# Order of the q and k turns in a fused attention and windowed-transformer kernel: q, q, k, k with q scaled ahead of k

## The chip, the cores and the metric

The kernel runs on one core of a Trainium2 chip. The metric is device time in microseconds (us). The engines are TensorE (PE for matmuls, PEld for the loads of the stationary operand), VectorE (DVE), ScalarE (ACT), GpSimd (POOL) and SyncE (SP, whose queue issues the DMAs). Each engine works through its own list of instructions in order; semaphores are all that ties the lists together.

## The reference, cut to what matters

The input is 2048 tokens of width 128, in float32. It is normalised and feeds two branches, whose results are added to it. The first is an attention over all tokens with 16 heads of width 8. The second, on which the change bears, is a stack of six layers, each a windowed attention followed by a gated MLP. Of one layer's attention:

```python
def attn_layer(x, Wqkv, qs, ksc, Wo):
    q, k, v = jnp.split(x @ Wqkv, 3, -1)      # 16 heads of 64
    q = l2norm(q) * qs
    k = l2norm(k) * ksc
    q = q * cos * scale + rotate_half(q) * sin * scale
    k = k * cos * inv + rotate_half(k) * sin * inv
    out = local_attention(q, k, v)            # windows of 32, one window back
    return out @ Wo
```

## The kernel before, in words

Part A, up to about 750 us, computes the attention over all tokens. Part B computes the six layers. It cuts the 2048 tokens into 16 tiles of 128, so it has 96 tiles in all (`END`), and a chunk is four tiles, 24 in all. Every engine has a loop over `u` in which each stage is called with the tile that is due: the loop is a software pipeline, written out by hand, and the order of the calls in it is the order of the engine's list. Tiles are counted from 0 over all layers here; tile t of the text is `u` in a function's own argument.

The way of a tile through q and k:
- `project` (L1325 and on, products at L1334 to L1336): PE multiplies the tile with a third of Wqkv, two banks of PSUM for each of q, k and v. The float32 product is made of three products of cut operands.
- `squares` (L754, ACT) squares the raw q or k, and `square_sums` (L1020, DVE) sums it by head. From these ACT and POOL form the reciprocal norms (L764 to L768, then POOL L634, L641, L643).
- `rotate_cos` (L1038) and `rotate_sin` (L1049, L1050), both DVE, read the raw q or k from PSUM. The last of them frees the bank pair of q or k (semaphore `q_out` or `k_out`).
- `rotated` (L652, POOL) adds the two parts in SBUF, and `normalise` (L660, POOL) multiplies by the reciprocal norm. It raises `q_scaled` or `k_scaled`.
- `turn` (L1360, PE) transposes the scaled q or k, 128 columns at a time: a call has four transposes, so a tile has four calls, q_turn0, q_turn1, k_turn0 and k_turn1. Each waits for `q_scaled` or `k_scaled` and for its PSUM bank.
- `turned_q` (L776) and `turned_k` (L785 into this tile's keys, L788 into the next tile's window back), both ACT, move the turned halves to SBUF, in the order q, q, k, k.
- `score` (L1376, L1381, PE) needs all four. DVE takes the maxima (L1069), ACT the 16 exponentials (L805, `exponentials`), DVE the sums (L1076) and their reciprocals (L1083), POOL scales (L614), DVE transposes blocks (L1061), SP moves them, and PE multiplies with v (`values`, L1397). ACT moves that result out (L796), and `output` (L1409, PE) multiplies with Wo.

In one round of PE's loop the turns belong to tile t = u - 2. Ahead of them stand the output product of tile t - 3 and the q and k products of tile t + 1. Behind them stands the v product of tile t + 1. `mean` (L1418, part of the MLP's layer norm) stands ahead of the last turn in one round in four: at tiles 6, 10, ... 94, and once more in the tail. The up products of a chunk (also L1334 to L1336, from `xl_cut`, whose low half is L1139 on DVE) follow the v product in the rounds of tiles 5, 9, ... The variance product (L1426) and the down product (L1448) follow it in the rounds of tiles 3, 7, ...

Banks of PSUM are shared between stages. `BANKS` gives the banks for even and odd tiles, and `bank_users` walks through the stages in PE's order, to say for each use whose reading out it must wait for:

```python
BANKS = {"q": ((4, 5), (4, 5)), "k": ((2, 3), (2, 3)), "v": ((0, 1), (4, 5)),
         "q_turn0": ((4,), (4,)), "q_turn1": ((1,), (5,)), "k_turn0": ((6,), (6,)),
         "k_turn1": ((0,), (7,)), "values": ((6, 7), (6, 7)), "output": ((7,), (7,)),
         "score": ((0, 1), (0, 1)), "mean": ((7,), (7,)), "var": ((4,), (4,)),
```

So q_turn0 always waits until DVE has read the raw q of the next tile (L1050). For an even tile, q_turn1 (bank 1) and k_turn1 (bank 0) wait for the exponentials of the tile before (L805), and the v product behind them (banks 4 and 5) waits for ACT's first reading of turned q. For an odd tile, q_turn1 (bank 5) waits for the same as q_turn0, and the v product (banks 0 and 1) waits for the exponentials.

POOL's round is: low half of x (L607), scaling of probabilities (L614), tables (L627), `rotated` of k, the reciprocal norms, `normalise` of k, `normalise` of q, `rotated` of the next tile's q.

Of the kernel before, what the change touches and what calls it, by code (L numbers as in the profile page):

```python
# [104 lines left out]
def tile(x):  # L105
    return x if 0 <= x < END else None


def chunk(x):
    c, r = divmod(x - 3, 4)  # L110
    return c if r == 0 and 0 <= c < CHUNKS else None


def dense_turn(x):
    g, r = divmod(x - 22, 8)
    return g if r == 0 and 0 <= g < NC else None


def late(x):
    c = chunk(x)  # L120
    return c if c is not None and c >= CHUNKS - NC else None
# [15 lines left out]
def banks_of(stage, unit):  # L137

    return (0, 1) if stage == "up2" and unit == CHUNKS - 2 else BANKS[stage][unit % 2]


def bank_users():

    users, last = {}, {}

    def take(stage, unit):
        if unit is not None:
            of = banks_of(stage, unit)
            users[stage, unit] = [last[b] for b in of if b in last]
            last.update({b: (stage, unit) for b in of})  # L150

    for u in range(FIRST, LAST):
        take("score", tile(u - 3))
        take("finish", late(u - 12))
        take("q", tile(u - 1))
        take("values", tile(u - 5))
        take("k", tile(u - 1))
        take("output", tile(u - 5))
        take("k_turn0", tile(u - 2))
        take("q_turn0", tile(u - 2))  # L160
        take("q_turn1", tile(u - 2))
        take("mean", chunk(u - 5))
        take("k_turn1", tile(u - 2))
        take("v", tile(u - 1))
        take("up0", chunk(u - 8))
        take("up2", chunk(u - 8))
        take("var", chunk(u - 6))
        take("down", chunk(u - 10))
        take("att", dense_turn(u))
        take("up1", chunk(u - 8))  # L170
    return users
# [18 lines left out]
def memory(nc, ctx, d):  # L190
# [79 lines left out]

    m.e_turn = exp_turns()
    m.users = bank_users()
    return m

# [9 lines left out]
def place(u):  # L284
    layer, i = divmod(u, NT)
    return layer, i, slice(i * P, (i + 1) * P)


def chunk_cols(g, skew=0):
    return slice(g * CH + skew, (g + 1) * CH + skew)  # L290
# [45 lines left out]
def wait_part_a(w, s):  # L336
    w.wait_ge(s["skew"], 2 * NC)
    w.wait_ge(s["pv"], H * NT * NC)
    for i in range(3):
        w.wait_ge(s[f"E_out{i}"], len(range(i, H * NT * NC + H, 3)))  # L340
    w.wait_ge(s["sc_max"], 2 * H * NT)
    w.wait_ge(s["o_ev"], H)
    w.wait_ge(s["ld_o0"], 16 * NC * H)
    w.wait_ge(s["ld_o1"], 16 * NC * H)
    w.wait_ge(s["z_low"], 2 * NC)
    w.wait_ge(s["idb"], 1)
    w.wait_ge(s["st_cut"], 32 * len(CUTS))
    w.wait_ge(s["cut"], 2 * len(CUTS))
# [250 lines left out]
def gpsimd_b(e, w, m, s):  # L599
    view = lambda a: a.rearrange("p (h d) -> p h d", h=H)  # L600

    def low_x(u):
        if u is None:
            return
        layer, i, c = place(u)
        w.wait_ge(s["x_hi"], u + 1)
        e.tensor_tensor(m.x_cut[u % 2][:, 1, :], m.stream[0][:, c], m.x_cut[u % 2][:, 0, :], ALU.subtract).then_inc(s["x_lo"], 1)  # L607

    def scale_probs(u):
        if u is None:  # L610
            return
        pb = m.pr[u % 2]
        w.wait_ge(s["sm_rec"], u + 1)
        e.tensor_tensor(pb[:, :, :, :], pb[:, :, :, :],  # L614
                        m.mxB[:, 2, :].unsqueeze(1).unsqueeze(3).to_broadcast([P, 2, H, WIN]), ALU.mult).then_inc(s["pnorm"], 1)

    def rotary(u):
        if u is None:
            return
        layer, st = u // NT, u % 2  # L620
        w.wait_ge(s[f"ld_rot{st}"], 16 * (u // 2 + 1))
        w.wait_ge(s[f"ld_gains{layer % 2}"], 96 * (layer // 2 + 1))
        w.wait_ge(s["rotq_c"], u - 1)
        w.wait_ge(s["q_out"], u - 1)
        w.wait_ge(s["rotk_c"], u - 1)
        w.wait_ge(s["k_out"], u - 1)
        e.tensor_tensor(m.rt[st][:, :, :], m.rot[st][:, :, :], m.gains[layer % 2][:, :, :], ALU.mult).then_inc(s["rt"], 1)  # L627

    def root_slope(u):
        if u is None:  # L630
            return
        c, t, r = [b[:, :] for b in m.rs[u % 2]]
        w.wait_ge(s["rB_sq"], u + 1)
        e.tensor_tensor(t, t, c, ALU.mult).then_inc(s["rB_t"], 1)  # L634

    def root_fix(u):
        if u is None:
            return
        c, t, r = [b[:, :] for b in m.rs[u % 2]]
        w.wait_ge(s["rB_t"], u + 1)  # L640
        e.tensor_scalar(t, t, -0.5, 1.5, ALU.mult, ALU.add).then_inc(s["rB_f"], 1)  # L641
        w.wait_ge(s["rB_f"], u + 1)
        e.tensor_tensor(r, r, t, ALU.mult).then_inc(s["rB_r"], 1)  # L643

    def rotated(u, i):
        if u is None:
            return
        n, tc = "qk"[i], m.tcs[u % 2][i]
        w.wait_ge(s[f"rot{n}_c"], u + 1)
        w.wait_ge(s[f"rot{n}_s"], u + 1)  # L650
        w.wait_ge(s[f"{n}_out"], u + 1)
        e.tensor_tensor(tc[:, :], tc[:, :], m.ts[i][:, :], ALU.add).then_inc(s[f"rot{n}"], 1)  # L652

    def normalise(u, i):
        if u is None:
            return
        n, tc = "qk"[i], view(m.tcs[u % 2][i][:, :])
        w.wait_ge(s[f"rot{n}"], u + 1)
        w.wait_ge(s["rB_r"], u + 1)
        e.tensor_tensor(tc, tc, m.rs[u % 2][2][:, i * H:(i + 1) * H].unsqueeze(2).to_broadcast([P, H, DH]),  # L660
                        ALU.mult).then_inc(s[f"{n}_scaled"], 1)

    wait_part_a(w, s)
    for i in range(2):
        e.memset(m.k_T[i][:, :, 0:WIN], 0.0).then_inc(s["zeroB"], 1)
    for u in range(FIRST, LAST):
        low_x(tile(u))
        scale_probs(tile(u - 3))
        rotary(tile(u))
        rotated(tile(u - 1), 1)  # L670
        root_slope(tile(u - 1))
        root_fix(tile(u - 1))
        normalise(tile(u - 1), 1)
        normalise(tile(u - 1), 0)
        rotated(tile(u), 0)


# [652 lines left out]
def tensor_b(e, w, m, s):  # L1330
# [20 lines left out]
    def turn(u, i, hf):  # L1351
        if u is None:
            return
        name = f"{'qk'[i]}_turn{hf}"
        bank = banks.one(name, u).rearrange("p (a b) -> p a b", b=P)
        w.wait_ge(s["k_scaled" if i else "q_scaled"], u + 1)
        banks.wait_free(w, name, u)
        for j in range(4):
            b = 4 * hf + j
            t = e.transpose(bank[:, j, :], m.tcs[u % 2][i][:, b * P:(b + 1) * P], m.ident[:, :])  # L1360
        t.then_inc(s[f"turn{i}{hf}"], 1)
# [50 lines left out]
    def mean(c):  # L1412
        if c is None:
            return
        layer, g = divmod(c, NC)
        w.wait_ge(s["y_out"], 4 * c + 4)
        banks.wait_free(w, "mean", c)
        e.matmul(banks.one("mean", c), m.ones[:, :], m.stream[1][:, chunk_cols(g)], start=True,  # L1418
                 stop=True).then_inc(s["mean_mm"], 1)

    def variance(c):
        if c is None:
            return
        w.wait_ge(s["lnsq"], c + 1)
        banks.wait_free(w, "var", c)
        e.matmul(banks.one("var", c), m.ones[:, :], m.lnb[:, :], start=True, stop=True).then_inc(s["var_mm"], 1)  # L1426
# [31 lines left out]
    def finish(c):  # L1458
        if c is None:
            return  # L1460
        bank = banks.one("finish", c).rearrange("p (j f) -> p j f", f=P)
        w.wait_ge(s["down_out"], c + 1)
        banks.wait_free(w, "finish", c)
        for j in range(CH // P):
            o = c % NC * CH + j * P
            t = e.transpose(bank[:, j, :], m.att[:, o:o + P], m.ident[:, :])
        t.then_inc(s["fin_T"], 1)

    for u in range(FIRST, LAST):
        score(tile(u - 3))  # L1470
        finish(late(u - 12))
        project(tile(u - 1), 0)
        values(tile(u - 5))
        project(tile(u - 1), 1)
        output(tile(u - 5))
        turn(tile(u - 2), 1, 0)
        turn(tile(u - 2), 0, 0)
        turn(tile(u - 2), 0, 1)
        mean(chunk(u - 5))
        turn(tile(u - 2), 1, 1)  # L1480
        project(tile(u - 1), 2)
        up_product(chunk(u - 8), 0)
        up_product(chunk(u - 8), 2)
        variance(chunk(u - 6))
        down_product(chunk(u - 10))
        dense_output(dense_turn(u))
        up_product(chunk(u - 8), 1)
# [62 lines left out]
```

## Time and profile before

| | |
|---|---|
| median of 3 runs | 2282.62 us (2280.07 to 2282.78) |
| the profiled execution | 2277.0 us |
| its span in the profile | 2275.2 us |
| PE, PEld busy | 92%, 57% |
| DVE, ACT, POOL busy | 87%, 78%, 58% |
| mean granted TensorE clock | 0.974 |
| from the first turn to the last (part B) | 760.5 to 2214 us |

The span is what the profiler saw from the first to the last instruction; the execution's own time is 1.8 us more. A row of a timeline gives the start (us from the span's start), the length in us, engine, line, operation, result and inputs, shape, and how many instructions are merged in it. A bracket gives the idle time of the engine ahead of it and what ended that. A merged row runs from the first start to the last end; matmuls overlap, so a row's end lies after the next row's start.

### The profile page before, as it was taken

To read this page: it belongs to the slowest core of one execution; us is meant where nothing else is said; L and a number is where in the kernel's file an instruction comes from. 1 tells how busy PE (TensorE), PEld (TensorE's weight loads), DVE (VectorE), ACT (ScalarE), POOL (GpSimd) and SP (SyncE) were. 2 spreads that over 40 slices of the span, in tenths; PEclk is the share of its full clock that TensorE was granted. 3 is DMA by queue.
4 is the path that set the end of the run, shared out by engine and by line. 5 is a ranking of instruction groups with operands and counts; after the bars stand their busy time and mean duration, and the time that the engine had idled before them with its cause. 6 is when DMAs were issued, how large, how long until landed. Compare 5 with 4: busy or idle time off the path is not lost. (4 is left out here: it accounts for less than half of the span.)

```text
span 2275.2 us, 69842 instructions
## 1 busy us (share of the span) xinstructions
PE 2103.4 (92%) x28313; PEld 1287.8 (57%) x28313; DVE 1984.4 (87%) x2379; ACT 1770.7 (78%) x4234; POOL 1311.7 (58%) x1084
## 2 busy tenths in 40 slices
PE   5999999999998689999999999999999999999986
PEld 2122222222221477777777777677777777777764
DVE  7999999999990788989898999888898999899984
ACT  3388888888887577878787888788787878788873
POOL 4201101111100788878787888787787878888870
PEclk8699999999999799999999999999999999999998
DMA  2322222221220233353434334443335333533331
GB/s 43 98 61 77 79 62 90 67 79 47 62 78 8 59 87 75 83 145 84 104 84 126 99 93 104 113 103 86 82 85 141 85 92 85 139 86 98 84 89 52
DMA packets 167798, 194.12 MB, mean 85 GB/s; under 512 B 87414, under 2 KB 107508, under 8 KB 167476
## 3 DMA queue, kind: packets, MB, share of 16 engines
q1 hardware_dynamic: 167220, 189.65, 32.0%
q8 instruction: 223, 3.65, 0.7%
q14 instruction: 99, 0.81, 0.1%
q10 hardware_dynamic: 256, 0.00, 0.0%
HBM read 56.98 MB, written 25.42 MB: 36 GB/s over the span
## 5 line engine op out<-in xcount | busy, mean ns | idle before, releaser
L988 DVE TENSOR_REDUCE mx<-S_ps 128x1 f32<-128x1024 f32 x512 | 601.7, 1219 | 25.5 <-PE S_ps L1288 20.0
L736 ACT ACTIVATE PT<-E_ps 128x512 f32<-128x512 f32 x1024 | 533.4, 603 | 102.3 <-PE E_ps L1297 99.8
L652 POOL TENSOR_TENSOR tc<-tc,ts 128x1024 f32<-128x1024 f32 x192 | 463.1, 2412 | 28.8 <-DVE ts L1050 28.2
L660 POOL TENSOR_TENSOR tc<-tc,rs 128x1024 f32<-128x1024 f32 x192 | 362.7, 1910 | 13.7
L1288 PE MATMUL S_ps<-KS,QS 48*128 48x512 bf16 x1024 | 321.2, 400 | 9.9 <-DVE mx L988 4.7
L805 ACT ACTIVATE pr<-B_ps,mxB 128x64 f32<-128x64 f32 x1536 | 323.8, 371 | 1.6 <-DVE mxB L1069 1.6
L1297 PE MATMUL E_ps<-QS,KS 64*128 64x512 bf16 x1024 | 317.5, 383 | 7.4 <-ACT PT L736 5.2
L594 POOL CAST w_cut_b<-w_raw_b 128x512 fp32r<-128x512 f32 (+1 forms) x48 | 27.6, 574 | 512.5 <-DMA w_raw_b<-in_Wqkv 380.0
L1334 PE MATMUL B_ps<-w_qkv,x_cut 128*128 128x512 f32 x576 | 259.8, 451 | 30.7 <-POOL x_cut L607 8.8
L1305 PE MATMUL O_ps<-PT,va 128*32 128x512 f32 x2048 | 274.1, 607 | 0.0
L1297 PEld LDWEIGHTS E_ps<-QS,KS 64*128 64x128 bf16 x1024 | 79.4, 94 | 338.5 <-ACT PT L736 257.9
L614 POOL TENSOR_TENSOR pr<-pr,mxB 128x1024 f32<-128x1024 f32 x96 | 183.8, 1915 | 138.3 <-DVE mxB L1083 138.3
L1038 DVE TENSOR_TENSOR tc<-B_ps,rt 128x1024 f32<-128x1024 f32 x192 | 234.8, 1223 | 29.9 <-ACT nrm L754 23.7
L754 ACT ACTIVATE nrm<-B_ps 128x1024 f32<-128x1024 f32 x192 | 208.1, 1084 | 37.2 <-PE B_ps L1336 36.7
L1020 DVE TENSOR_REDUCE ss<-nrm 128x16 f32<-128x1024 f32 x192 | 232.0, 1208 | 0.0
L1335 PE MATMUL B_ps<-w_qkv,x_cut 128*128 128x512 f32 x576 | 231.6, 402 | 0.0
L1336 PE MATMUL B_ps<-w_qkv,x_cut 128*128 128x512 f32 x576 | 230.9, 401 | 0.3 <-issue 0.3
L1360 PE MATMUL B_ps<-ident,tc 128*128 128x128 f32 x1536 | 204.9, 277 | 22.4 <-POOL tc L660 10.8
L1397 PE MATMUL B_ps<-xy,vs 128*64 128x64 f32 x3072 | 196.3, 228 | 19.7 <-issue 9.0
L1360 PEld LDWEIGHTS B_ps<-ident,tc 128*128 128x128 f32 x1536 | 173.1, 142 | 52.3 <-issue 19.7
L1397 PE MATMUL B_ps<-xy,v 128*64 128x64 f32 x3072 | 192.4, 225 | 9.1 <-issue 9.1
L1397 PEld LDWEIGHTS B_ps<-xy,vs 128*64 128x64 f32 x3072 | 168.1, 140 | 57.4 <-issue 57.2
(181 smaller groups left out, 3971.3 us busy)
## 6 DMA issues: line engine op xcount, KB each, us to landing
xy<-pc SPq DMA_DIRECT2D x768, 64.0 KB, 2.0
vs<-v SPq DMA_DIRECT2D x96, 384.0 KB, 3.7
Wqkv_cut<-w_cut_b SPq DMA_DIRECT2D x72, 256.0 KB, 2.4
w_qkv<-Wqkv_cut SPq DMA_DIRECT2D x36, 512.0 KB, 7.3
rot<-in_rot SPq DMA_DIRECT2D x96, 128.0 KB, 2.6
vs<-v SPq DMA_DIRECT2D x96, 128.0 KB, 3.8
w_raw_b<-in_Wqkv SPq DMA_DIRECT2D x36, 256.0 KB, 2.9
W_cut<-w_cut_b SPq DMA_DIRECT2D x24, 170.5 KB, 2.5
```

The source lines that it names most:

```text
L652: e.tensor_tensor(tc[:, :], tc[:, :], m.ts[i][:, :], ALU.add).then_inc(s[f"rot{n}"], 1)
L660: e.tensor_tensor(tc, tc, m.rs[u % 2][2][:, i * H:(i + 1) * H].unsqueeze(2).to_broadcast([P, H, DH]), ALU.mult).then_inc(s[f"{n}_scaled"], 1)
L736: e.activation(m.PT[n % NPT][:, :], turns.bank("probs", n)[:, :], ACT.Exp).then_inc(turns.sem("probs", n), 1)
L805: a = e.activation(pb[:, :, h, :], sc[:, h, :, :], ACT.Exp, bias=m.mxB[:, 0, h:h + 1], scale=1.0)
L988: e.tensor_reduce(m.mx[h % 2][:, i, hf:hf + 1], m.S_ps[n % 2][:, :, :], AX.XY, ALU.max).then_inc(s["sc_max"], 1)
L1038: e.tensor_tensor(view(m.tcs[u % 2][i][:, :]), raw, wide(m.rt[u % 2][:, 2 * i, :], DH), ALU.mult).then_inc(s[f"rot{n}_c"], 1)
L1288: mm = e.matmul(m.S_ps[n % 2][:, c, :], m.QS[sl][rows, i * P:(i + 1) * P], m.KS[sl][rows, k:k + CH], start=True, stop=True)
L1297: e.matmul(turns.bank("probs", n)[:, :], m.KS[sl][rows, j * P:(j + 1) * P], m.QS[sl][rows, chunk_cols(c)], start=True, stop=True).then_inc ...
L1305: e.matmul(m.O_ps[VC * c:VC * (c + 1), :], m.va[:, j, h, :], m.PT[n % NPT][:, :], start=(j == 0), stop=(j == NT - 1)).then_inc(s["pv"], 1)
L1334: e.matmul(bank, left[0], right[0], start=True, stop=False)
L1360: t = e.transpose(bank[:, j, :], m.tcs[u % 2][i][:, b * P:(b + 1) * P], m.ident[:, :])
L1397: mm = e.matmul(bank[at, j, :, b, :], v[:, d:d + DH], m.xy[u % 2][:, b, :, par * NP + j, :], start=(b == 0 and j % (NP // 2) == 0), stop=T ...
```

## The change

The two calls of q's turns move ahead of the first of k's turns in PE's loop, and in the walk that assigns the waits for banks. In POOL's loop the scaling of q moves ahead of the scaling of k. No instruction is added or removed, no bank is changed, and ACT's order of reading out stays as it is. `normalise(u, 0)` is q, `turn(u, 0, half)` is q.

```diff
--- before.py
+++ after.py
@@ -156,9 +156,9 @@
         take("values", tile(u - 5))
         take("k", tile(u - 1))
         take("output", tile(u - 5))
-        take("k_turn0", tile(u - 2))
         take("q_turn0", tile(u - 2))
         take("q_turn1", tile(u - 2))
+        take("k_turn0", tile(u - 2))
         take("mean", chunk(u - 5))
         take("k_turn1", tile(u - 2))
         take("v", tile(u - 1))
@@ -670,8 +670,8 @@
         rotated(tile(u - 1), 1)
         root_slope(tile(u - 1))
         root_fix(tile(u - 1))
+        normalise(tile(u - 1), 0)
         normalise(tile(u - 1), 1)
-        normalise(tile(u - 1), 0)
         rotated(tile(u), 0)
 
 
@@ -1473,9 +1473,9 @@
         values(tile(u - 5))
         project(tile(u - 1), 1)
         output(tile(u - 5))
-        turn(tile(u - 2), 1, 0)
         turn(tile(u - 2), 0, 0)
         turn(tile(u - 2), 0, 1)
+        turn(tile(u - 2), 1, 0)
         mean(chunk(u - 5))
         turn(tile(u - 2), 1, 1)
         project(tile(u - 1), 2)
```

## Rows read from the trace of the kernel before

**Rows 1.** Busy time by stretch: length, PE, PEld, DVE, ACT, POOL, granted clock, DMA share, GB/s.
```profile
760.00:2214.00 1454.00, 1358.46 (x23648) 1075.91 (x23649) 1297.29 (x1668) 1176.59 (x3093) 1186.47 (x949) 0.99 0.38 96
```
**Rows 2.** The turns' line L1360: duration, and PE's idle time ahead of it by what ended it.
```profile
L1360 PE MATMUL B_ps<-ident,tc x1536: 272/273/477, 760.5 to 2213.8; 128*128 128x128 f32 x192
...
  POOL tc L660: 30.3, 41
...
  ACT pr L805: 12.8, 37
```
**Rows 3.** Timeline, odd tile 43: the turns, POOL's scaling, the v product.
```profile
1416.32 1.90 POOL L660 TENSOR_TENSOR tc<-tc,rs 128x1024 f32<-128x1024 f32 x1
...
1417.91 1.91 PE L1360 MATMUL B_ps<-ident,tc 128*128 128x128 f32 x16
...
1419.58 0.48 PE L1334 MATMUL B_ps<-w_qkv,x_cut 128*128 128x512 f32 x1
```
**Rows 4.** Timeline, even tile 42 with the mean product: from the turns to the scores.
```profile
1404.65 1.83 PE L1360 MATMUL B_ps<-ident,tc 128*128 128x128 f32 x12
...
1405.82 0.42 PEld L1360 LDWEIGHTS B_ps<-ident,tc 128*128 128x128 f32 x4 [0.37 <-ACT pr L805]
...
1407.17 0.60 PE L1360 MATMUL B_ps<-ident,tc 128*128 128x128 f32 x4
...
1407.53 0.48 PE L1334 MATMUL B_ps<-w_qkv,x_cut 128*128 128x512 f32 x1
...
1408.11 0.77 ACT L785 ACTIVATE k_T<-B_ps 128x512 f32<-128x512 f32 x1
...
1408.59 0.55 ACT L788 ACTIVATE k_T<-B_ps,carry 128x128 f32<-128x128 f32 x1
...
1408.79 0.39 PE L1336 MATMUL B_ps<-w_qkv,x_cut 128*128 128x512 f32 x1
...
1409.28 0.39 PE L1376 MATMUL B_ps<-mask_bf,pick_bf 64*128 64x512 bf16 x2
```
**Rows 5.** The turns of the first (tile 6) and the last (tile 94) such round.
```profile
847.33 1.84 PE L1360 MATMUL B_ps<-ident,tc 128*128 128x128 f32 x12
...
2197.64 1.83 PE L1360 MATMUL B_ps<-ident,tc 128*128 128x128 f32 x12
```
**Rows 6.** Timeline, even tile 44 without the mean product: first turns, v product.
```profile
1435.78 0.60 PE L1360 MATMUL B_ps<-ident,tc 128*128 128x128 f32 x4
...
1438.35 0.50 PE L1334 MATMUL B_ps<-w_qkv,x_cut 128*128 128x512 f32 x1 [0.28 <-ACT q_T L776]
```
**Rows 7.** Timeline, odd tile 33: turns, POOL, the v product, xl_cut and the up product.
```profile
1265.71 0.60 PE L1360 MATMUL B_ps<-ident,tc 128*128 128x128 f32 x4
...
1266.37 2.38 POOL L652 TENSOR_TENSOR tc<-tc,ts 128x1024 f32<-128x1024 f32 x1
...
1267.75 0.48 PE L1334 MATMUL B_ps<-w_qkv,x_cut 128*128 128x512 f32 x1
...
1267.99 1.31 DVE L1139 TENSOR_TENSOR xl_cut<-xl,xl_cut 128x512 fp32r<-128x512 f32 x1
...
1269.36 0.19 PEld L1334 LDWEIGHTS B_ps<-xl_cut,w 128*128 128x128 f32 x1 [0.40 <-DVE xl_cut L1139]
```
**Rows 8.** Timeline, odd tile 21: DVE's reading of q, turns, the up product.
```profile
1078.23 0.67 DVE L1050 TENSOR_TENSOR ts<-B_ps,rt 128x512 f32<-128x512 f32 x1
...
1079.05 1.50 PE L1360 MATMUL B_ps<-ident,tc 128*128 128x128 f32 x12 [0.61 <-POOL tc L660]
...
1082.06 0.19 PEld L1334 LDWEIGHTS B_ps<-xl_cut,w 128*128 128x128 f32 x1 [0.55 <-DVE xl_cut L1139]
```
**Rows 9.** All DVE's xl_cut instructions: duration in ns, shortest, median, longest.
```profile
L1139 DVE TENSOR_TENSOR xl_cut<-xl,xl_cut x24: 681/1248/2005, 895.9 to 2258.2; 128x512 fp32r<-128x512 f32 x24
```
**Rows 10.** Timeline, PE at the start of a layer, after tile 30; PE's turns of tile 95.
```profile
1227.60 0.47 PE L1334 MATMUL B_ps<-w_qkv,x_cut 128*128 128x512 f32 x1 [0.62 <-DMA w_qkv<-Wqkv_cut]
...
2212.59 1.53 PE L1360 MATMUL B_ps<-ident,tc 128*128 128x128 f32 x12 [0.40 <-POOL tc L660]
```

## The prediction

> **What bounds the kernel now.** I read the page first. PE is busy 92% of the span, but DVE, ACT and POOL are at 87, 78 and 58%, so no single share settles it, and I went by stretches. The change touches only the stretch from 760 to 2214 us. There PE is busy 1358 of 1454 us at a granted clock of 0.99, DVE 1297, ACT 1177, POOL 1186 [rows 1]. PE has 96 us of gaps, one us a tile, and of those only a part stands ahead of the turns. The view of line L1360 says what part: 30.3 us in 41 gaps ended by POOL's scaling, and 12.8 us in 37 gaps ended by ACT's exponentials [rows 2]. The first sum is what the change can win, the second what it can make longer. Then I went through the timeline, tile by tile.
>
> An undisturbed tile shows the scale. Its 16 turns stand in one row of 1.91 us without a gap, one turn takes 0.27 us, so they start (1.91 - 0.27) / 15 = 0.11 us apart and a call of four costs 0.44 us [rows 2, 3]. POOL's second scaling ends at 1416.32 + 1.90 = 1418.22, that is 0.31 us after the first turn, and q's first call is due 0.44 us after it. So k_turn0 already covers the whole wait for q here. Tiles 3, 7, ... 91 look like this or have POOL still earlier.
>
> **The change part by part.** It adds no work: four calls of 0.44 us and two scalings of 1.90 us stay what they are. Nothing moves on SP, DVE or ACT, and no DMA. On POOL, q is ready one scaling (1.90 us) sooner and k as much later. What is queued behind both, the next tile's `rotated`, starts at the same time. So everything is decided by which of three releases comes last on PE: the scaling, DVE's reading of the next raw q, or ACT's exponentials.
>
> *Odd tiles where q waits for POOL.* In tile 33 POOL's second scaling ends where `rotated` (L652) begins behind it, at 1266.37 or 0.66 us after the first turn, and q_turn0 waits for it. The v product starts at 1267.75, 2.04 us after the first turn at 1265.71; undisturbed it is 1419.58 - 1417.91 = 1.67 [rows 3, 7]. With q first, the second scaling is needed 0.88 us after the first turn instead of 0.44, so this gap of 0.37 goes. I find 13 such tiles, all in the rounds of the up products (first tile 13, last tile 89), worth 4.3 us together at 0.03 to 0.48 us each. But what is late next? In tile 33 the up product waits for `xl_cut`, which ends at 1267.99 + 1.31 = 1269.30, while PE had been idle 0.40 us in its weight loads [rows 7]. That DVE instruction takes 0.68 us at its shortest and 1.25 at the median [rows 9], and it is long where POOL's L652 lies across it: here L652 ends at 1268.75 and DVE 0.55 us later. Neither of the two moves with the order of the scalings. So I take nothing for these tiles, with 4.3 us as the other bound: the v product comes 0.37 us sooner and the up product at the same time.
>
> The Trainium skill has a rule for this, in "SBUF — State Buffer", section "SBUF: two separate sides": a DVE instruction with two SBUF inputs and a GpSimd instruction that reads SBUF take one port pair by an exclusive lock, and the later one blocks until the other is done. The trace agrees in that the DVE instruction ends a fixed 0.55 us behind POOL's. By the rule these 13 tiles give nothing; without it, all 4.3 us.
>
> *Odd tiles where q waits for DVE too.* In tiles 21, 73 and 93 q_turn0 waits 0.61 us on PE's row [rows 8]. The gap bears POOL's name, but DVE's reading of the next q ends as late, at 1078.23 + 0.67 = 1078.90, 0.15 us before q's turns start. With q first, q_turn0 still waits for DVE, and k_turn0, which ran under this wait, now runs behind: +0.44 us on the v product. The up product behind it had been waiting for `xl_cut` already: 12 turns from 1079.05 are 1.31 us, the v product's six products 1.50 (1407.53 to 1409.03 in tile 42, below), so PE was free at 1081.86 and started at 1082.06 [rows 8]. These 0.20 us absorb nearly half; I take 0.2 us each, +0.6 us for three, between 0 and 1.3. Among the first three tiles, where the pipeline fills, tiles 1 and 2 have long waits of this kind; I take +0.5 us for the three, between 0 and 3 x 0.44 = 1.3.
>
> *Even tiles.* These carry the sum. q_turn1 (bank 1) waits for the exponentials. In tile 42 the weight load of q_turn1 starts at 1405.82 after an idle 0.37 us ended by ACT, and the first 12 turns take 1.83 us instead of 0.27 + 11 x 0.11 = 1.48 [rows 4]. The exponentials do not depend on the turns: they end 1.12 us after the first turn in nearly all even tiles. With q first, q_turn1 is due 0.44 us after the first turn, not 0.88. It still starts at 1405.82, and k_turn0 comes behind it and no longer under the wait. So the calls end 0.44 us later.
>
> What this costs depends on what stands behind. Without the mean product (tiles 4, 8, ...) the v product waits 0.28 us on PE's row for ACT's first reading of turned q: it starts at 1438.35, 2.57 us after the first turn at 1435.78, [rows 6]. If q_turn1 starts 1.17 us after the first turn, as in tile 42, three calls bring PE to the v product at 1.17 + 3 x 0.44 = 2.49, still under 2.57. I take 0 for these, because ACT's chain (exponentials, squares, q) does not move; without that cover it would be 0.44 us for each of 24.
>
> With the mean product, 23 tiles, there is no such cover: mean stands between q_turn1 and k_turn1, and the v product follows k_turn1 at once, at 1407.53 [rows 4]. The first and the last of them show the same 1.84 and 1.83 us [rows 5]. The v product comes 0.44 us later, at 1407.97. Behind it come the scores, and they start at 1409.28, 0.14 us after ACT's last reading of turned k (1408.59 + 0.55 = 1409.14). PE was free at 1409.03, one product (0.24 us) after the start of the last, 1408.79. After the change PE is free at 1409.47. ACT's second reading of k, now at 1408.11, needs k_turn1, which ends at 1407.77 + 0.44 = 1408.21, so ACT is 0.12 us late and would let the scores go at 1409.40. PE is the later: the scores start some 0.20 us later, 0.20 and not 0.44. This is the term I trust most in kind, and its bounds are 0 and 0.44. From the scores on PE runs without a gap to `values`, and DVE, ACT and POOL behind it wait for PE, so the 0.20 us stays in the time. Not everywhere: at the start of each new layer, after tiles 14, 30, 46, 62 and 78, the q product waits for its weights (0.62 us after tile 30 [rows 10]), whose DMA was started before the turns, and after three others (54, 58, 94) `values` is late for other reasons. That leaves 15 tiles: 15 x 0.20 = 3.0 us.
>
> *The last tile.* Tile 95 has q waiting 0.40 us for POOL on PE's row, on the chain that ended last, with no up product behind it [rows 10]: -0.4 us.
>
> **Sum:** 3.0 + 0.6 + 0.5 - 0.4 = +3.7 us. The profiled execution took 2277.0 us with a span of 2275.2; it would become 2280.7. The median of the runs, 2282.6, lies 5.6 us above the profiled one, and I put the same difference on it: 2286.3 us, +0.16%. A measurement of this kernel tells about 0.2% (4.6 us) from no change, so the likeliest verdict is no change, leaning to slower.
>
> **The rivals.** (1) *The full 0.44 us, slower.* If the 0.44 us of the 23 mean tiles goes through whole, because the scores do not have the slack I read from ACT's last reading, the sum is 23 x 0.44 + 1.3 + 1.3 - 0.4 = +12.3 us, 2294.9. It decides at 0.31 us a tile (with 15 tiles, above +4.6 us in all; with 23 tiles at 0.20 us). For it: PE is the fullest engine, and the gaps that absorb are few. Against: the 0.25 us between PE's being free and the scores stand in the timeline of every such tile. Chance 0.27.
>
> (2) *The gains come through, faster.* If `xl_cut` does not hold PE, because it ends sooner once the up product is asked for sooner, the 13 tiles give 4.3 us, and if ACT's slack swallows the 23 tiles wholly, nothing stands against it: -4.3 - 0.4 = -4.7, 2277.9 us. For it: 30.3 us of gaps bear POOL's name. Against: most of them are in the filling of the pipeline and under `xl_cut`. Chance 0.10.
>
> (3) *No effect beyond tenths.* The turns shift inside their round and every stage behind them is released by ACT or DVE as before: 0 to +1 us, 2283. Chance 0.13. My forecast has 0.50.
>
> Gaps ended by nothing that the profile shows (19.7 us before the turns in the view of L1360) can shift by a few us with any reordering. They widen every case.
>
> **How the numbers follow.** Faster by over 0.2%: rival 2 is at the bound, 0.10, with 0.02 from scatter: 0.12. Slower: rival 1, 0.27, and a tail of the forecast, 0.06: 0.33. Within: 0.55. The range takes in the forecast, rival 3 and most of rival 1, whose median case with partial cover is near 2292: 2280 to 2293.
>
> **What would show it.** In the changed profile tile 42's kind has the first four turns, a gap of about 0.6 to 0.8 us ended by ACT's L805, then eight turns, mean, four turns, and the v product about 3.3 us after the first turn instead of 2.88. The scores follow 4.8 us after the first turn instead of 4.63. The idle time of L1360 ended by L805 grows from 12.8 to some 30 us, and that ended by POOL's L660 falls by 10 us or more. In rounds like tile 33's the v product moves up 0.37 us and the up product not at all. The forecast is wrong if the distance of the scores grows by 0.4 us or by nothing, or if the up product follows the v product.

## The result, and the profile after

| | before | after |
|---|---|---|
| median of 20 runs each, same chip | 2281.1 us (2276.42 to 2283.28) | 2287.73 us (2277.76 to 2299.18) |
| profiled execution | 2277.0 us, span 2275.2, clock 0.974 | 2296.88 us, span 2295.1, clock 0.968 |

The ratio is 1.0028, with a 95% interval of 1.0017 to 1.004: +6.4 us, between 3.9 and 9.1. The point forecast was 2286.3 us and the range 2280 to 2293, so the time lies inside. The median is slower by a little more than the 0.2% that the text called the least that can be told, and the interval reaches to both sides of that bound.

Two things need care. The profiled execution is one of the slowest of the changed kernel, 9 us above its median. And its runs spread over 21 us where those of the kernel before spread over 7. So I read in it only distances inside single tiles, and took a second profile of both kernels (below). Busy time by stretch, [rows 1] of the changed kernel, same columns:

```profile
760.00:2234.00 1474.00, 1362.31 (x23649) 1086.02 (x23650) 1296.91 (x1668) 1178.06 (x3094) 1185.90 (x949) 0.98 0.37 95
```

The stretch is 20 us longer. No engine has work to match: PE's busy time grew 4 us, DVE's, ACT's and POOL's by 1.5 us at most. The other 16 us are gaps of PE. Two more lines of the view of L1360 before, the one of [rows 2]:

```profile
  issue: 19.7, 59
...
  DVE ts L1050: 7.2, 9
```

The same view of the changed kernel shows who releases the turns now:

```profile
L1360 PE MATMUL B_ps<-ident,tc x1536: 272/273/446, 761.9 to 2233.2; 128*128 128x128 f32 x192
...
  ACT pr L805: 42.5, 69
  issue: 41.1, 72
  DVE ts L1050: 23.7, 20
  POOL tc L660: 0.6, 2
```

POOL's 30.3 us are down to 0.6, so the change does what it says. ACT's 12.8 us have become 42.5, DVE's 7.2 have become 23.7, and those that nothing in the profile ends, 19.7, have become 41.1. These sums are larger than PE's idle time: the view adds the gaps on the row of the matmuls (PE) to those on the row of the weight loads (PEld), so that one wait can stand in it twice. Row by row, of POOL's 30.3 us before 10.8 stand on the matmuls' row and 19.6 on the loads'. Of ACT's 42.5 us after, 16.9 stand on the matmuls' row, and all 41.1 us of "issue" on the loads'. Next the timeline of tile 42, the answer to [rows 4]:

```profile
1411.61 0.60 PE L1360 MATMUL B_ps<-ident,tc 128*128 128x128 f32 x4
...
1412.78 1.09 PE L1360 MATMUL B_ps<-ident,tc 128*128 128x128 f32 x8 [0.57 <-ACT pr L805]
...
1413.71 1.02 PE L1418 MATMUL B_ps<-stream,ones 128*128 128x512 f32 x2
...
1414.57 0.60 PE L1360 MATMUL B_ps<-ident,tc 128*128 128x128 f32 x4
...
1414.92 0.48 PE L1334 MATMUL B_ps<-w_qkv,x_cut 128*128 128x512 f32 x1
...
1415.20 0.64 ACT L785 ACTIVATE k_T<-B_ps 128x512 f32<-128x512 f32 x1
...
1415.70 0.40 ACT L788 ACTIVATE k_T<-B_ps,carry 128x128 f32<-128x128 f32 x1
...
1416.50 0.39 PE L1376 MATMUL B_ps<-mask_bf,pick_bf 64*128 64x512 bf16 x2
```

Four turns, a gap of 0.57 us ended by the exponentials, eight turns, the mean product, four turns. The v product starts 3.31 us after the first turn (2.88 before). The scores start 1416.50 - 1411.61 = 4.89 us after it (4.63 before): 0.26 us later. ACT's second reading of k (L785) starts 3.59 us after the first turn, 0.13 later than before, but it is as much shorter (0.64 instead of 0.77 us). Its last reading ends at 1416.10, 4.49 us after the first turn and exactly as far as before. The scores start 0.40 us behind that end, where it was 0.14: now PE is the last, with the v product's last matmul at 1416.17.

### The profile page after: what moved, and what is told of

Same layout as the page of the kernel before. It is cut to its first block and busy times, and to the rows that moved or that the text cites. A ratio compares the mean times of both kernels' runs of the same rounds, so it can differ in the third digit from the quotient of the medians.

```text
span 2295.1 us, 69842 instructions
## 1 busy us (share of the span) xinstructions
PE 2107.0 (92%) x28313; PEld 1297.1 (57%) x28313; DVE 1984.1 (86%) x2379; ACT 1771.7 (77%) x4234; POOL 1311.2 (57%) x1084
## 3 DMA queue, kind: packets, MB, share of 16 engines
q8 instruction: 223, 3.65, 0.7%
## 5 line engine op out<-in xcount | busy, mean ns | idle before, releaser
L652 POOL TENSOR_TENSOR tc<-tc,ts 128x1024 f32<-128x1024 f32 x192 | 463.3, 2413 | 37.3 <-DVE ts L1050 36.8
L1334 PE MATMUL B_ps<-w_qkv,x_cut 128*128 128x512 f32 x576 | 261.0, 453 | 24.3 <-POOL x_cut L607 8.9
L1360 PE MATMUL B_ps<-ident,tc 128*128 128x128 f32 x1536 | 198.6, 277 | 41.2 <-DVE ts L1050 23.7
L1360 PEld LDWEIGHTS B_ps<-ident,tc 128*128 128x128 f32 x1536 | 172.4, 142 | 67.4 <-issue 41.1
```

What stands on the lines that cost most here:

```text
L1334: e.matmul(bank, left[0], right[0], start=True, stop=False)
```

## The experiments

Twelve kernels ran, each timed in five rounds beside the kernel before on the same chip. Theories 1 and 2 stood at the start, the third came before e5. **Theory 1**: the order costs time in the 23 tiles with the mean product, where q_turn1 and not k_turn0 stands at ACT's exponentials. **Theory 2**: it costs where PE's gaps ahead of the turns, once split by k_turn0, become one long gap, and the granted clock falls behind it. **Theory 3**: beside the cost in the mean tiles, part of the loss is in stalls inside the scores that the profile puts down to nothing, and where these fall hangs on where the code of PE lies.

### One half undone, one half alone

**e1**: PE in the order q, k, q, k; POOL as in the change. Here and in e3 the walk that assigns the waits for banks follows PE's order.

```diff
         turn(tile(u - 2), 0, 0)
-        turn(tile(u - 2), 0, 1)
         turn(tile(u - 2), 1, 0)
+        turn(tile(u - 2), 0, 1)
```

> Changed kernel, but PE turns q, k, q, k, so that k_turn0 again runs while q_turn1 waits for the exponentials; POOL's order stays q, k. Theory 1 (the loss is the cover that q_turn1's wait lost in the 23 mean tiles, plus the first tiles): the scores of tile 42 start 4.64 us after the first turn again instead of 4.89, values 7.97 instead of 8.22, the steps of 0.25 us vanish, and the time comes back to before, +0 to +1.5 us. Theory 2 (most of the loss is half-clock stretches behind longer single gaps ahead of q_turn0, which waits for DVE in either order): +4 to +8 us, with 10 or more half-clock stretches and a spread of the runs of over 10 us, as in the changed kernel.

Measured: 2282.58 us, ratio 1.0015 (1.0001 to 1.0029), +3.4 us. Timeline of tile 42 in e1:

```profile
1405.83 1.82 PE L1360 MATMUL B_ps<-ident,tc 128*128 128x128 f32 x12
...
1407.00 0.42 PEld L1360 LDWEIGHTS B_ps<-ident,tc 128*128 128x128 f32 x4 [0.37 <-ACT pr L805]
...
1408.35 0.60 PE L1360 MATMUL B_ps<-ident,tc 128*128 128x128 f32 x4
...
1410.46 0.39 PE L1376 MATMUL B_ps<-mask_bf,pick_bf 64*128 64x512 bf16 x2
```

With k_turn0 back under the wait the scores stand 4.63 us behind the first turn again. The 0.26 us are thus the lost cover of q_turn1, and about half of the loss goes with them. The rest, e1's +3.4 us, lies in neither theory's range (0 to 1.5 and 4 to 8). Its runs stay within 10 us (2276.9 to 2286.89).

**e2**: the changed kernel, with q_turn1 of even tiles in bank 5, which the exponentials do not use.

```diff
-         "q_turn0": ((4,), (4,)), "q_turn1": ((1,), (5,)),
+         "q_turn0": ((4,), (4,)), "q_turn1": ((5,), (5,)),
```

> Changed kernel with q_turn1 of even tiles in bank 5 instead of bank 1, so that it waits for DVE's reading of q (done before) and not for the exponentials; k_turn1 still waits for them. Theory 1: q, q, k run without a gap (0, 0.44, 0.87), the v product of tile 42 waits for ACT's second reading of q at about 3.05 us, and the scores start at 4.6 to 4.7 us instead of 4.89: +0 to +1.5 us against before. Theory 2: no difference to the changed kernel, +4 to +8 us.

Measured: 2290.65 us, ratio 1.0051 (1.0031 to 1.0071), +11.6 us. This missed: it should have cured the tiles, and it is slower than the change itself. The timeline of e2 for tile 42:

```profile
1411.12 1.47 PE L1360 MATMUL B_ps<-ident,tc 128*128 128x128 f32 x12
...
1414.28 0.47 PE L1334 MATMUL B_ps<-w_qkv,x_cut 128*128 128x512 f32 x1 [0.39 <-ACT q_T L776]
```

and the idle time ahead of the products' line L1334 in e2, by what ended it:

```profile
  ACT q_T L776: 53.4, 83
```

Before, that line had 15.7 us in 38 gaps. The wait for the exponentials has gone (12 turns in 1.47 us), but the v product of an even round writes banks 4 and 5. Bank 5 now holds turned q, and v waits for ACT's second reading of it, in tiles with and without mean (in tile 4, without, v starts 3.17 instead of 2.58 us after the first turn). The scores stand at 4.73 instead of 4.63 us in the mean tiles and at 4.74 instead of 4.64 us in tile 4. I had looked at who writes bank 1 and not at who writes bank 5 next.

**e3** has the new order on PE alone, **e4** on POOL alone.

```diff
 e3, PE
-        turn(tile(u - 2), 1, 0)
         turn(tile(u - 2), 0, 0)
         turn(tile(u - 2), 0, 1)
+        turn(tile(u - 2), 1, 0)
 e4, POOL
+        normalise(tile(u - 1), 0)
         normalise(tile(u - 1), 1)
-        normalise(tile(u - 1), 0)
```

> Only PE's half of the change: PE turns q, q, k, k, but POOL still scales k first, so q_turn0 needs the second scaling at once. Theory 1: in tiles 3, 7, ... q_turn0 waits 0.3 us for POOL (+0.3 us each, 23 tiles), in 13 tiles of the up products the whole of 0.5 to 0.7 us, of which the wait for xl_cut takes part: with the 0.25 us of the mean tiles, +10 to +17 us against before. Theory 2: the same gaps, and more half-clock stretches still: over +17 us.

> Only POOL's half of the change: q is scaled first, but PE still turns k first, so k_turn0 needs the second scaling at once. Theory 1: mean tiles as before (scores at 4.64 us), +0.3 us in each of tiles 3, 7, ..., about +0.25 us in the 13 tiles of the up products: +6 to +11 us. Theory 2: as in theory 1 by the gaps, and a spread of the runs of over 10 us.

Measured: e3 2292.49 us, ratio 1.0057 (1.0038 to 1.0077), +13.0 us, as expected; e4 2282.17 us, 1.0017 (1.0005 to 1.0029), +3.9 us, less than expected. Idle time ahead of L1360, of e3 and then of e4:

```profile
  POOL tc L660: 47.6, 50
  ACT pr L805: 42.6, 67
```

```profile
  POOL tc L660: 55.7, 84
...
  ACT pr L805: 16.8, 54
```

Either half alone makes POOL the last releaser more often than the 30.3 us of before. In e4, PE's first turn is still k's, now scaled last: 25 us more of gaps bear POOL's name, and the time grows by 3.9. On the matmuls' row alone POOL's gaps grow by 12.1 us (22.9 after 10.8) and DVE's fall by 6.0 (1.2 after 7.2), so about half of it is a wait that only changed its name. In e3, ACT's 42.6 us alone equal those of the change: they come with PE's order.

### New order in the tiles with mean only, and in the others only

```diff
+def q_first(t):
+    return chunk(t - 3) is not None
...
+def turn_order(t):
+    return ("q_turn0", "q_turn1", "k_turn0") if q_first(t) else ("k_turn0", "q_turn0", "q_turn1")
...
-        turn(tile(u - 2), 1, 0)
-        turn(tile(u - 2), 0, 0)
-        turn(tile(u - 2), 0, 1)
+        for stage in turn_order(u - 2):
+            turn(tile(u - 2), "qk".index(stage[0]), int(stage[-1]))
```

This is **e5**; POOL and the list of banks follow the same function, and **e6** has `is None` for the other 73 tiles.

> The new order (PE q, q, k, k and POOL q first) in the 23 tiles with the mean product alone, the old order in the other 73. Theory 1 (the loss sits in the cover that q_turn1's wait lost in the mean tiles): scores at 4.89 and values at 8.22 us there, +3 to +5 us against before, that is about all of the change's loss but the first tiles. Theory 3 (the loss sits elsewhere: in the filling of the pipeline, in DVE's release of q_turn0 and in the stalls inside the scores that it moves): the same distances in the timeline, but less than half of the change's +6.4 us, under +3 us.

> The complement: the new order in the 73 tiles without the mean product, the old one in the 23 with it. Theory 1: 0 to +1.5 us, values of tile 42 at 7.97 us. Theory 3: +3 to +6 us, with the stalls at the scores of tile 4 (about 825 us) and tiles 50 to 56 that the changed kernel's trace has and the one before has not.

Measured: e5 2285.18 us, ratio 1.0025 (1.0009 to 1.0041), +5.7 us (2.1 to 9.3); e6 2283.74 us, 1.0016 (1.0002 to 1.003), +3.6 us (0.5 to 6.8). Tile 42 in e5 and then in e6 (their lines are numbered 7 higher):

```profile
1405.16 0.60 PE L1367 MATMUL B_ps<-ident,tc 128*128 128x128 f32 x4
...
1406.34 1.09 PE L1367 MATMUL B_ps<-ident,tc 128*128 128x128 f32 x8 [0.58 <-ACT pr L812]
...
1410.06 0.39 PE L1383 MATMUL B_ps<-mask_bf,pick_bf 64*128 64x512 bf16 x2
```

```profile
1408.63 1.84 PE L1367 MATMUL B_ps<-ident,tc 128*128 128x128 f32 x12
...
1413.28 0.39 PE L1383 MATMUL B_ps<-mask_bf,pick_bf 64*128 64x512 bf16 x2
```

4.90 us in e5, 4.65 in e6. Theory 1 gives 23 x 0.26 = 6.0 us, and e5 has 5.7. The granted clock is not what makes it: its median over the runs is 0.973 in e5 and in the kernel beside it. But a stall of 1.38 us in tile 50, of the kind shown below, is in e5's profile too, so the 5.7 us need not be the mean tiles' alone. And e6, where the order predicts nothing or a small gain, is not at zero. What it loses does not repeat from tile to tile. Measured from scores to scores, each kind of tile (by its place in the chunk) differs from before by a median of 0.02 us or less, while single tiles differ by -1.3 to +3.4 us.

### The same kernels once more, and moved in the instruction stream

Because the loss in single tiles looked accidental, both kernels were run again (**e7** the change, **e8** the kernel before), and both with 64 or 128 satisfied waits on PE ahead of the loop, which move its later code and change no order.

```diff
+    for _ in range(64):
+        e.wait_ge(s["fold_mm"], 9)
     for u in range(FIRST, LAST):
         score(tile(u - 3))
```

> The changed kernel once more, for a second profile beside the first (span 2295.1 us) and for runs on the same chip: +4 to +9 us. Theory 1: its distances in the mean tiles are 4.89 and 8.22 us again. Theory 3: the stalls of 1.8 to 2 us inside the scores at 825 and between 1540 and 1630 us stand at the same places again, so they belong to the order and are not chance.

> The kernel before once more, for a second profile: 0 us, within 0.1%. Theory 3: none of the stalls named for the changed kernel at 825 us, and at most two between 1540 and 1630 us; if they come and go, the profile of one run can't carry that theory.

> The changed kernel with 64 waits on a semaphore long reached put ahead of part B on PE (32 instructions in the program), so that all of PE's later code sits further back; nothing else. Theory 3 (beside the 0.26 us in the mean tiles, the rest of the loss is stalls inside the scores that hang on where PE's instruction loads fall): the stalls at tile 4 (about 824 us) and tile 50 (about 1540 us) vanish or move to other tiles, and the median moves by 2 us or more, either way; the mean tiles keep 4.89 and 8.22 us. Theory 1 (the order alone): the same stalls at the same tiles, the median within 1.5 us of 2287 us.

> As before it with 128 such waits (64 instructions). Theory 3: a third pattern of stalls, with tile 4 and tile 50 not both stalled, and a median 2 us or more from one of the other two. Theory 1: the same as the changed kernel within 1.5 us.

> The kernel before with the same 64 waits. Theory 3: its median moves by 2 us or more from 2279 us, most likely upwards, as its own placing is among the better ones; the mean tiles keep 4.64 and 7.97 us, and the changed kernel with the same padding is 4 to 8 us slower than it. Theory 1: within 1.5 us of 2279 us.

> The kernel before with 128 such waits. Theory 3: as for 64, another pattern; over the three placings the difference between the orders averages some 6 us, 23 tiles by 0.26 us. Theory 1: within 1.5 us of 2279 us, and the changed kernel 6 to 8 us above it in every placing.

| placing | old order | new order | difference |
|---|---|---|---|
| as it is | e8 2278.93, 0.9995 (0.9984 to 1.0007) | e7 2286.94, 1.0036 (1.002 to 1.0053) | +8.0 (4 to 14) |
| 64 waits | e11 2283.65, 1.002 (1.0003 to 1.0036) | e9 2287.56, 1.0022 (1.0011 to 1.0033) | +3.9 (-1 to 7) |
| 128 waits | e12 2287.31, 1.0021 (1.0008 to 1.0035) | e10 2292.19, 1.005 (1.0038 to 1.0062) | +4.9 (3 to 8) |

The last column is the difference of the medians, with 95% of what it gives when the 5 to 12 runs of each are drawn again. By the ratios it would be +9.3, +0.5 and +6.6 us. The new order costs 5.6 us by the mean of the medians' differences and 5.5 by that of the ratios, near the 6.0 of the mean tiles, but the second row by itself doesn't tell it from zero, and the third rests on only five runs of e10. Part of the first row is the clock: the median granted clock is 0.971 in e7's runs and 0.973 in e8's, and e7's own runs go by 2.2 us for 0.001, so some 4 of the 8.0 us, an estimate, go with it. Moved by 64 waits, the change went from a ratio of 1.0036 to 1.0022, by 128 to 1.005, that is -3.2 and +3.2 us, though its median moved by only +0.6 and by +5.2; theory 3 asked for 2 or more. The old order, moved, is itself 4.6 to 4.8 us slower by its ratios. The waits at the head are not what costs: the first turn of tile 0 starts at 760.1 and 760.3 us in e11 and e12, and at 760.5 and 759.6 in the two profiles of before. What was moved costs later.

Where, the timelines tell. Tile 4's scores on PE, of the change, of e7 and of e8:

```profile
823.02 1.38 PE L1381 MATMUL B_ps<-k_T,q_T 64*32 64x64 f32 x116
...
826.26 0.33 PE L1381 MATMUL B_ps<-k_T,q_T 64*32 64x64 f32 x12 [1.85 <-issue]
```

```profile
821.65 1.38 PE L1381 MATMUL B_ps<-k_T,q_T 64*32 64x64 f32 x116
...
824.74 0.33 PE L1381 MATMUL B_ps<-k_T,q_T 64*32 64x64 f32 x12 [1.70 <-issue]
```

```profile
821.01 1.48 PE L1381 MATMUL B_ps<-k_T,q_T 64*32 64x64 f32 x128
```

In both runs of the change PE stops after the same 116 of 128 score matmuls for 1.70 to 1.85 us, and the view names nothing that ends the gap. e3 stops there too (1.58 us), and e2 one matmul earlier (2.08). The kernel before doesn't stop there in either profile, nor do e1, e4 to e6 or e9 to e12. Tile 50 has a second such place, after matmul 114 (1.87 us in the change, 1.97 in e7), and so have e3 (1.36) and e5 (1.38), which have the new order in this tile; before, e1, e2, e4 and e6 have none there, and e9, the new order moved by 64 waits, has none:

```profile
1536.42 1.09 PE L1360 MATMUL B_ps<-ident,tc 128*128 128x128 f32 x8 [0.57 <-ACT pr L805]
...
1540.46 1.49 PE L1381 MATMUL B_ps<-k_T,q_T 64*32 64x64 f32 x128
```

In e9 the 0.57 us ahead of the turns stay and the stall is gone. Summed over the kernel, PE's waits of this kind within L1381 (us, times, longest), of the change and of e8:

```profile
PE B_ps L1381 <- issue: 13.7, 9, 2.0
```

```profile
PE B_ps L1381 <- issue: 9.3, 6, 1.9
```

e7 has 12.9 us and the first profile of before 9.1, so some 4 us of the profiled difference lie here. Most such places belong to no order: tiles 52, 54 and 55 stall after matmuls 125, 124 and 126 in the change and in the kernel before, in both profiles of each. e8, of which at most two between 1540 and 1630 us were expected, has four. The moved kernels have their stalls in new places, most of them the same in both orders, among them the products' line L1334. There e11 has its longest (e9 has 4.30 us at this place, e10 and e12 have 5.30 and 5.56 us at another place of this line; the longest in the two profiles of before is 3.16):

```profile
1725.80 0.59 PE L1334 MATMUL B_ps<-w_qkv,x_cut 128*128 128x512 f32 x1 [5.29 <-issue]
```

**What ends the stalls** can be read from the DMA packets. One packet of the instruction queue falls into 823.5 to 826.5 us of the change:

```profile
q8 instruction: 1, 0.02, 2.3%
```

It runs from 823.54 to 824.65 us, and PE goes on at 826.26, 1.61 us after its end. In e7 PE goes on 1.44 us after the end of such a packet. In e8 the packet ahead of this matmul ended at 818.54, 3.6 us before PE came to it, and the next one starts only behind it; the same holds for before, e1 and e4 to e6, by 2.5 to 4.0 us. In tile 50 the packet ends 0.1 to 0.8 us after PE has come to the place in the four kernels that stall after matmul 114, and 3.4 us or more ahead in the other six whose code isn't moved. And it holds everywhere: of the 14 profiles' 235 gaps of over 0.4 us on PE's matmul row between 760 and 2215 us that the view calls "issue", each ends 1.20 to 1.67 us after the end of a packet of the instruction queue, though such packets come only every 7.7 us on average. So the stalls fit a wait for instructions whose packet came late. Why it comes late in one order or placing and not in another stays open.

These 235 gaps add up to 27.5 and 25.0 us in the two profiles of before, 31.7 and 28.4 in those of the change, 27.3 in e9, 30.4 in e10, 32.3 in e11 and 29.5 in e12. With 6.0 us for the mean tiles, the difference between the orders would be 9.4 us from e8 to e7, where the spans differ by 10.4, and 1.0 from e11 to e9, where they differ by 1.0. From the first profile of before to that of the change it would be 10.2 of 19.9, and from e12 to e10 6.9 where 3.4 were measured: there something else changed too.

**Theory 2** has one clear place, tile 40. The turns on PE and the next 4.5 us in the change:

```profile
1380.68 2.66 PE L1360 MATMUL B_ps<-ident,tc 128*128 128x128 f32 x16 [2.39 <-DVE ts L1050]
```

```profile
1381.00:1385.50 4.50, 4.50 (x21) 3.80 (x19) 4.42 (x9) 3.14 (x7) 3.89 (x3) 0.62 0.45 119
```

and the stretch of before that answers to it:

```profile
1373.50:1378.00 4.50, 2.88 (x18) 2.34 (x18) 4.42 (x8) 4.50 (x15) 3.94 (x3) 1.00 0.74 197
```

PE sits idle 2.39 us in one piece for DVE's reading of raw q. Then the granted clock is 0.62 on average, part of it at 1.2 GHz and part at 2.4, and 16 turns take 2.66 us. Before, k_turn0 stood inside the wait and left 1.69 us of it ahead of q, and the clock stayed at 1.00. From tile 39's first turn to tile 41's it is 2.6 us longer, 0.90 of which is a stall in tile 40's scores, and the next tile gives 1.1 of it back. e7, e6 and e2 show the same (gaps of 2.59, 2.54 and 2.51 us, granted clock 0.67 over e7's 1376.00 to 1380.50), e5 and e8, with the old order here, do not. But e1 and e3 had gaps of 2.26 and 2.69 us in this place and kept 1.00. In e9 and e10 the gap itself was shorter (1.47 and 1.28 us), and the clock stayed up. In e11, with the old order, the half clock comes later in the tile, behind a stall of 1.91 us in the scores. So the place fits the theory, and neither the order nor the length of the gap decides it.

As a theory of the whole loss it falls, for e1 kept the long waits for DVE and lost half of the loss. Between 785 and 2215 us the clock record has 1.2 GHz for 20 and 24 us in the two profiles of before, 44 and 25 in those of the change, and 34 and 40 in e11 and e12, whose order is the old one. So moving the code, too, came with more time at 1.2 GHz.

## Why the prediction was right, and where it was off

**Tiles with mean: right in place and kind, too small.** The text took +0.20 us for the scores and got +0.26. It had ACT 0.12 us late, with its second reading of k at the scores. ACT's second reading did start 0.13 us later, but it was 0.13 us shorter, and its chain kept its end at 4.49 us. PE is the later one, as the text had it, and the scores start 0.26 us later. The text let them start the moment PE is free; in the changed trace they start 0.09 us behind that (last product 1416.17 + 0.24, scores 1416.50), and this is about what the step was short by. The larger error is the count. I let the time of five layer starts and three others be absorbed, and took 15 tiles: 3.0 us. Ten tiles with nothing else in them each have a period longer by 0.21 to 0.26 us in both pairs of profiles (before and the change, e8 and e7). All 23 at 0.26 us make 6.0 us, and e5, which changes only these, measured +5.7. So the mis-sized term is 15 x 0.20 = 3.0, which is 23 x 0.26 = 6.0 to the accuracy that e5 gives, 2.1 to 9.3, with tile 50's stall in it. Whether each of the eight excepted tiles pays the 0.26 can't be read: in the layer starts and in tiles 54 and 94 the period moves by more than 1 us between kernels of the same order (tile 46: +2.4 and +1.2 us in the two profiles of the change, +3.3 in e11).

**Tiles without mean: zero, right.** Tile 44, [rows 6], after the change:

```profile
1443.79 1.94 PE L1360 MATMUL B_ps<-ident,tc 128*128 128x128 f32 x16 [0.62 <-DVE ts L1050]
...
1445.57 0.50 PE L1334 MATMUL B_ps<-w_qkv,x_cut 128*128 128x512 f32 x1
```

q_turn0 comes first and waits for DVE, a wait that k_turn0 used to fill. The text didn't have that wait, but its cover held. Counted from the end of the output product ahead of the turns, v starts at 2.40 us (2.41 before), and over all 23 tiles of this kind the median of the scores' start is 4.48 us in both. The bound of 0.44 us each for 24 tiles didn't come.

**Tiles with an up product: almost no gain, right in the sum, not in its reason.** Tile 33, [rows 7], after the change:

```profile
1270.94 1.91 PE L1360 MATMUL B_ps<-ident,tc 128*128 128x128 f32 x16
...
1271.28 2.39 POOL L652 TENSOR_TENSOR tc<-tc,ts 128x1024 f32<-128x1024 f32 x1
...
1272.61 0.48 PE L1334 MATMUL B_ps<-w_qkv,x_cut 128*128 128x512 f32 x1
...
1273.24 0.98 DVE L1139 TENSOR_TENSOR xl_cut<-xl,xl_cut 128x512 fp32r<-128x512 f32 x1
...
1274.28 0.19 PEld L1334 LDWEIGHTS B_ps<-xl_cut,w 128*128 128x128 f32 x1 [0.45 <-DVE xl_cut L1139]
```

The v product starts 1.67 us after the first turn instead of 2.04, the 0.37 us of the text. PE then still waits for `xl_cut`. That ends at 1274.22, again 0.55 us behind POOL's L652, which ends at 1273.67. Counted from the first turn, the up product starts at 3.34 us instead of 3.65, so here it followed the v product, which was a sign against the forecast. The text held that L652 doesn't move with the order. It did: it starts 0.34 us after the first turn instead of 0.66, and DVE's instruction, which ends 0.55 us behind it, came to its end sooner and was shorter (0.98 instead of 1.31 us). Tiles 65 and 81 are like it, in e7 as well. Measured from the scores ahead, the 13 up products start 1.0 us sooner in sum in the change and 0.7 in e7, of 4.3, and these three tiles make 1.0 in both. Even that isn't the tile's own order: e5 has it in tile 33 with the old order (3.30 us), and e6 doesn't with the new one (3.65). Rival 2, -4.7 us, is out.

That xl_cut's instruction is tied to POOL's is shown. In the 14 profiles it starts 245 times while L652 runs, and in 238 it ends 0.54 to 0.55 us after L652, whether it took 0.68 us or 2.0. Where no instruction of POOL lay across its start, it took 0.68 to 0.69 us. This is what the lock of the Trainium skill ("SBUF — State Buffer", "SBUF: two separate sides") describes, and the traces agree.

**Tiles 21, 73, 93: +0.6, measured about zero.** Tile 21, [rows 8], after the change:

```profile
1083.62 1.94 PE L1360 MATMUL B_ps<-ident,tc 128*128 128x128 f32 x16 [1.05 <-DVE ts L1050]
...
1086.62 0.19 PEld L1334 LDWEIGHTS B_ps<-xl_cut,w 128*128 128x128 f32 x1
```

q waits 1.05 us for DVE instead of 0.61 for POOL, as told, and all 16 turns follow. The up product starts 1086.62 - 1083.62 = 3.00 us after q's first turn, and 3.01 before: its wait of 0.55 us took the whole 0.44. I had let it absorb only 0.20, which left 0.24.

**The ends.** Tile 95 has its 16 turns in one row of 1.91 us, without the 0.40 us of [rows 10]: -0.4 as told. The first three tiles, +0.5, can't be told: tile 3 starts at 803.4 and 800.3 us in the two profiles of before, at 802.7 and 802.5 after.

**What the sum lacked.** The text had a sentence that gaps ended by nothing in the profile can shift by a few us, and no term for it. Of the remainder, the stalls such as those of tiles 4 and 50 are 4.2 and 3.4 us in the two pairs of profiles, and tile 40's half clock is a part. e6 has +3.6 us without any changed mean tile, but its stalls add up to 27.0 us, only 0.8 above the mean of before's two profiles, so most of its loss is not explained. The kernel before, moved by 64 or 128 waits, shows 4.6 and 4.8 us. The reading of [rows 2] was also too wide: "what the change can win" was put at 30.3 us, of which only 10.8 stand on the matmuls' row. The forecast of 2286.3 came this near partly by luck: it was too small by 3.0 us in the mean tiles and by the stalls, and too large by 0.6 in three tiles and by putting the start at 2282.6, the median of three runs, where twenty gave 2281.1. Rival 1, 0.44 us in every mean tile, is out in its mechanism, though its threshold (23 tiles at 0.20 us) was passed by 23 tiles at 0.26. Rival 3, at most +1 us, lies below the measured interval (3.9 to 9.1).

**Open.** Why the packets of the instruction queue come late in some places. What made e1 (+3.4 us) and e6 (+3.6) slower, with 23.5 and 27.0 us of stalls against 27.5 and 25.0 before. Why e6, with the change's order in tiles 0 to 5, has no stall in tile 4. Why the change's runs spread 21 us in one set and 15 in e7, against 11 in e8. What e2 lost beyond the 0.1 us of each even tile, which make some 5 of its 11.6 us. No version tried is faster than the kernel before.

## What to carry to other kernels

In a hand-written order, first find which instruction stands under each wait, and ask of a swap what will stand there instead: four turns moved out from under a wait cost what the next slack doesn't take, and that slack has to be read per kind of round, then counted in all of them. When an engine's buffer is moved to avoid one wait, look who writes the new one next. And before a difference of 0.2 to 0.3% is given to an edit's order, run both orders at two or three other placings of the code: here moving alone was worth 4.6 and 4.8 us, the edit 6.4.

## What was not expected of the hardware

- PE stalled for 1.85 and 1.70 us after the same matmul (number 116 of 128 in tile 4) in two profiles of one program and not in others. Every such gap of over 0.4 us, 235 in 14 profiles, ended 1.20 to 1.67 us after a packet of the instruction queue had landed. Moving the code by 64 or 128 waits, with tile 0 starting within 1 us of where it had, changed a kernel of 2281 us by 4.6 and 4.8 us.
- A single PE gap of 2.39 us was followed by a granted clock of 0.62 over 4.5 us, where with 1.69 us of the wait left ahead of q the clock stayed at 1.00. In e3 a gap of 2.69 us in the same place was followed by 1.00, so the length of the gap doesn't settle it.
- DVE's xl_cut instruction, 0.68 us by itself, ended 0.54 to 0.55 us after POOL's L652 in 238 of the 245 cases in which it started under it.
- Among the runs of one program the time went with the mean granted clock: 2299.18 us at 0.969 and 2277.76 at 0.975 for the change.
